# Row sums and reciprocals of a banded attention: products with ones against accumulating exponentials and transposed reciprocals

## The reference, cut to what matters

```python
def _L1_attn_ref(hidden_states, Wq, bq, Wk, bk, Wv, bv, Wo, bo):
    ...
    scores = jnp.einsum('bhtd,bhtwd->bhtw', q, kb) / scaling
    scores = jnp.where(valid[None, None], scores, -jnp.inf)
    probs = jax.nn.softmax(scores, axis=-1)
    ctx = jnp.einsum('bhtw,bhtwd->bhtd', probs, vb)
    ctx = ctx.transpose(0, 2, 1, 3).reshape(B, T, H * D)
    attn_output = ctx @ Wo.T + bo
    return attn_output
...
x = _layernorm(x + _L1_attn_ref(x, L1_attn_Wq, ...), axis=-1)
```

## Time and profile before

| | us |
|---|---|
| median of 3 runs | 878.39 |
| lowest, highest | 877.84, 883.13 |
| profiled execution, its own time | 879.82 |
| its span, first to last instruction | 878.0 |

### The profile page before, as it was taken

The page is one execution under the profiler, slowest core; times in us unless marked ns, Lnnn a source line. Parts: engine busy times, 40 slices in busy tenths (PEclk is TensorE's granted clock), DMA queues, the critical chain, the costliest instruction groups (busy, mean ns, idle before and its releaser), DMA issues.

```text
span 878.0 us, 20713 instructions
## 1 busy us (share of the span) xinstructions
PE 792.1 (90%) x7995; PEld 610.7 (70%) x7995; DVE 656.2 (75%) x1973; ACT 488.1 (56%) x1509; POOL 358.2 (41%) x604
## 2 busy tenths in 40 slices
PE   6888899988988889999988899999998899999992
PEld 4556777766666677766766778876766788877781
DVE  5363688687587878779667688789678788889576
ACT  3016335585646444577655554478656554578563
POOL 0358302304666532401685641311676632300655
PEclk9779989999989999999999999999999899999996
DMA  7892000000434100000126200000154100000001
GB/s 226 229 346 74 1 2 1 2 3 28 133 146 161 33 2 2 1 2 15 56 101 223 90 19 3 1 3 2 55 194 165 51 11 2 2 2 2 1 2 37
DMA packets 22994, 53.31 MB, mean 61 GB/s; under 512 B 3808, under 2 KB 9600, under 8 KB 22896
## 3 DMA queue, kind: packets, MB, share of 16 engines
q1 hardware_dynamic: 22896, 51.99, 17.9%
HBM read 48.67 MB, written 3.31 MB: 59 GB/s over the span
## 4 chain that ended last, share of the span: by engine, by line
PE 29%; DVE 10%; POOL 5%; ACT 4%; issue 2%; ACTq 0%; DVEq 0%; POOLq 0%
PE psum L441 6%; PE psum L436 6%; PE psum L478 5%; PE psum L621 2%; PE psum L643 2%; PE psum L634 2%; PE psum L464 2%; ACT x L701 1%; POOL rstd L1195 1%; DVE bn L937 1%; PE psum L471 1%; POOL xplus L1202 1%; PE psum L431 1%; PE psum L539 1%; PE psum L565 1%
## 5 line engine op out<-in xcount | busy, mean ns | idle before, releaser
L701 ACT ACTIVATE x<-res,ez,rstd 100x256 f32<-100x256 f32 x160 | 86.8, 593 | 67.4 <-POOL ez L1198 67.3
L1193 POOL TENSOR_SCALAR ve<-mv 100x2 f32<-100x2 f32 x96 | 22.2, 231 | 203.5 <-DVE mv L940 200.0
L478 PE MATMUL psum<-eT,ctx 128*128 128x100 f32 x768 | 101.2, 289 | 1.5 <-DVE eT L961 1.4
L478 PEld LDWEIGHTS psum<-eT,ctx 128*128 128x128 f32 x768 | 97.3, 205 | 3.7 <-DVE eT L961 2.7
L464 PE MATMUL psum<-ctxT,qT 128*100 128x361 f32 x256 | 84.1, 470 | 2.4 <-ACT qT L695 1.5
L695 ACT ACTIVATE eT<-psum 100x400 f32<-100x400 f32 (+3 forms) x128 | 61.8, 496 | 41.6 <-PE psum L471 18.2
L805 ACT ACTIVATE work<-psum,mx 100x100 f32<-100x100 f32 x256 | 67.4, 363 | 26.5 <-DVE mx L1104 26.2
L1177 POOL TENSOR_TENSOR kT<-cell,kT 100x722 f32<-100x722 f32 x12 | 20.6, 1719 | 137.9 <-ACT cell L675 137.9
L695 ACT ACTIVATE xT<-psum 128x400 f32<-128x400 f32 (+2 forms) x80 | 35.6, 447 | 70.7 <-PE psum L521 27.8
L811 ACT ACTIVATE work<-psum,mx 100x100 f32<-100x100 f32 x256 | 68.7, 386 | 8.6 <-DVE mx L1107 8.6
L1195 POOL TENSOR_TENSOR rstd<-ve,minus_half 100x2 f32<-100x2 f32 x96 | 69.7, 726 | 8.0
(11 more groups left out here) (241 smaller groups left out, 2007.7 us busy)
## 6 DMA issues: line engine op xcount, KB each, us to landing
ctx<-in_ctx SPq DMA_DIRECT2D x16, 768.0 KB, 7.0
ctxT<-in_ctxT SPq DMA_DIRECT2D x16, 722.0 KB, 5.4
cell<-in_cell SPq DMA_DIRECT2D x12, 282.0 KB
seq<-in_seq SPq DMA_DIRECT2D x12, 282.0 KB
x<-in_x SPq DMA_DIRECT2D x16, 200.0 KB
out<-vs SPq DMA_DIRECT2D x16, 200.0 KB
eT<-agent_rows SPq DMA_DIRECT2D x12, 200.0 KB
work<-in_x SPq DMA_DIRECT2D x4, 400.0 KB
```

Source lines behind the costliest of these rows:

```text
L478: last = e.matmul(bk[b][:, c * S:(c + 1) * S], s.ctx[:, b, j, c * P:(c + 1) * P], s.pT[:, b, j, :], start=j == 0, stop=j == S2C - 1)
L701: e.activation(dst[0:S, b, :], s.res[0:S, b, :], ACT.Identity, scale=s.rstd[:, b:b + 1], bias=s.shift[:, b:b + 1]).then_inc(*act.up(f"x{b}"))
```

## The change

The row sums are no longer made by PE. Each of the eight exponentials of an item now accumulates its row sum beside its output (`accum_out` into `s.den`). DVE takes the reciprocal of 100x8, POOL spreads it over 128 columns (`s.rspread`, which lies in the first half of `s.xT`), PE transposes that into bank 1, and DVE copies it to `s.xT[:, 1]`, from where the product L1116 takes it. The eight products with `sums` and the reciprocal of 128x100 go, as do the tile and its memsets. POOL's pieces for the four spreads stand between the stage's row addition and the masks of the next turn. The pieces are merged in new orders on all five engines: every string of ORDER is new.

```diff
-        sums = sb("sums", [S, 2, 2 * DH])
...
+                s.rspread = s.xT[0:S, :, :].rearrange("p c t -> p (c t)")[:, 0:P]
...
@@ tensor_turns, local
+                    e.wait_ge(*pool(f"re{i}", t))
+                    e.wait_ge(*dve(f"eT{i}", t))
+                    e.transpose(bk[1][:, 0:S], s.rspread, ident[0:S, 0:S]).then_inc(*pe.up(f"rt{i}"))
                     e.wait_ge(*act(f"eT{i}", t))
-                    e.wait_ge(*dve(f"eT{i}", t))
-                    for bank in range(2):
-                        for j in range(2):
-                            for r in range(ROWS):
-                                h = 2 * r + j
-                                last = e.matmul(bk[bank][32 * r:32 * r + 32, 0:S],
-                                                sums[:, j, :] if bank else s.v[0:S, b, c * HQ + h, :],
-                                                s.eT[0:S, h * S:(h + 1) * S], start=j == 0, stop=j == 1, skip_group_check=True)
+                    for j in range(2):
+                        for r in range(ROWS):
+                            h = 2 * r + j
+                            last = e.matmul(bk[0][32 * r:32 * r + 32, 0:S], s.v[0:S, b, c * HQ + h, :],
+                                            s.eT[0:S, h * S:(h + 1) * S], start=j == 0, stop=j == 1, skip_group_check=True)
                     last.then_inc(*pe.up(f"av{i}"))
...
@@ scalar_turns, local (and the same for heads 4 to 7)
                         last = e.activation(s.e[:, h, :], bk[0][0:S, h % 4 * S:(h % 4 + 1) * S], ACT.Exp,
-                                            bias=s.mx[0:S, h:h + 1])
+                                            bias=s.mx[0:S, h:h + 1], accum_out=s.den[0:S, h:h + 1])
...
@@ vector_turns, local
+                    e.wait_ge(*act(f"exb{i}", t))
+                    e.reciprocal(s.rden[0:S, 0:HQ], s.den[0:S, 0:HQ]).then_inc(*dve.up(f"rd{i}"))
                     e.wait_ge(*pe(f"trb{i}", t))
                     e.tensor_copy(s.eT[0:S, 4 * S:8 * S], bk[1][0:S, 0:4 * S]).then_inc(*dve.up(f"eT{i}"))
                     yield
+                    e.wait_ge(*pe(f"rt{i}", t))
+                    e.tensor_copy(s.xT[:, 1, 0:S], bk[1][:, 0:S]).then_inc(*dve.up(f"rT{i}"))
                     e.wait_ge(*pe(f"av{i}", t))
-                    e.reciprocal(s.xT[:, 0, 0:S], bk[1][:, 0:S]).then_inc(*dve.up(f"rd{i}"))
-                    e.wait_ge(*dve(f"rd{i}", t))
-                    e.tensor_tensor(s.aT[:, c, b * S:(b + 1) * S], bk[0][:, 0:S], s.xT[:, 0, 0:S], ALU.mult).then_inc(
+                    e.wait_ge(*dve(f"rT{i}", t))
+                    e.tensor_tensor(s.aT[:, c, b * S:(b + 1) * S], bk[0][:, 0:S], s.xT[:, 1, 0:S], ALU.mult).then_inc(
                         *dve.up(f"aT{i}"))
...
@@ gpsimd_turns, behind add_row of local, ahead of masks_product
+                for i in range(NB * NC):
+                    spread(s.gpsimd["local"], f"re{i}", s.vector["local"](f"rd{i}", t), s.rspread, S, HQ)
+                    yield
```

More of the change, by code:

```diff
@@ L70 @@
     "pick": "gates gath selT q k v hs0 hs tr0 tr1 av fo sc0 sc1",
-    "local": "xT q k v0 v1 " + " ".join(f"s{i} tra{i} trb{i} av{i}" for i in range(NB * NC)) + " out0 out1",
+    "local": "xT q k v0 v1 " + " ".join(f"s{i} tra{i} trb{i} rt{i} av{i}" for i in range(NB * NC)) + " out0 out1",
     "second": "xT q s0 s1 pT0 pT1 av0 av1 out0 out1",
@@ L89 @@
     "pick": "z0 z1 gp gt tie0 tie1 rk0 rk1 pk0 pk1 kT vs1 mx0 su0 mx1 su1 sm0 sm1 rd eT1 aT " + NORM,
-    "local": "k0 k1 k2 k3 v1 " + " ".join(f"ma{i} mb{i} eT{i} rd{i} aT{i}" for i in range(NB * NC)) + " " + NORM,
+    "local": "k0 k1 k2 k3 v1 " + " ".join(f"ma{i} mb{i} rd{i} eT{i} rT{i} aT{i}" for i in range(NB * NC)) + " " + NORM,
     "second": "mx0 nb0 mx1 nb1 pT0 rs aT1 " + NORM,
@@ L99 @@
     "pick": "zero re ve rstd nm0 nm1",
-    "local": "xb ve rstd nm0 nm1",
+    "local": "xb " + " ".join(f"re{i}" for i in range(NB * NC)) + " ve rstd nm0 nm1",
     "second": "xb prod qb ve rstd nm0 nm1",
@@ L850, in vector_agents @@
             e.memset(minus_half[:, :], -0.5)
-            for j in range(2):
-                for k in range(2):
-                    e.memset(sums[:, j, k * DH:(k + 1) * DH], float(j == k))
             e.memset(token_w, 0.0)
@@ L1415 @@
[L1415 to L1423 removed]
+        "ABCDABBCACBAADCBDABABACADBACBBDCDCCADDCDBDAAACBAABCBAADBCBACABDBACBCDBCDCABDDCADCABDACDABADABDCACBAC"
@@ new lines @@
+        "BABBBCDADCDCCCCBABACDADDADAADDCACBAABBBBBBDCBDCACABACADCCCCCDBAADBABBDACDDDDDABBCACCBBDCABDCDDCBCABD"
+        "CDACDADBACADBADBADCABCBDCACBCBDBDDAACBCDCCBADADBDABCBCDAABCABDBDCAABDDCCACABCDBDBCDABADCACBDCABDAAAA"
+        "ACDBCBDBCBBBCCADBDCACDCCDDDDDDBBCCDD"),
+    "DVE": (
+        "ABBDCCDDCAABAABBCADCBAACDBDABACABCDBCDDCCBAACDAABDBAADAABABBCCBBBABCDCCCDCCBDCDDADDDADAACABADCBCBBAD"
+        "ACCBBACDBBDCACBDCBAACBCBCDADCDABDCAABCBCACADBACADBDDBBCDBDDDAAACDACAABADBBADBBDBCCABCACBCCDDBDAACADB"
+        "DCDDCBABCBDAABDABACCABCDCACBABBCAADDBCBDCAABCDBAADBDCADBDBCDACBCCBDCCCDBDDDCADDDAACADBDABCABCACBCDBA"
+        "BCDBCABCCADDBADABDABCDBAADABCCDCDBABBCADAACDCBBDCBBCDAAADCCCDBDBAABADDDABBABCACADCBBCDBDCCBAADCDACDC"
+        "ADAABBBCDABDAACBCBCDAABCBCCBDDCCADACBDAABDAADBABDBDCCDBCBBACBCDDCCCBDDCDADDDCADAADBCBBABACABCCBADBAC"
+        "DBCDDABCAABCDDBBADCAADCABDCBCABDADBDACACBDCDCBBCBAADCDACCAAABBBADDADBDBBCCABCABCCDBCDADBAACDCDDACAAC"
+        "BBBDDAADBADCBCCABACBCBCBACDADCDABCADAADBDABBDBDBCCBBDACCBDCCDCCBDCDADDADDACADBADBACBBCAACCBDDBBCABDC"
+        "DAADCBCDBABCBADDAAABCDCBCBBDACADDCACBDBDCBCDDACACAADAADBBBDACCABCBBACBDDCCDBDDDBCDCDCD"),
@@ new lines @@
+    "ACT": (
+        "ABBBCACDBCAABAADBCABACCADDDDBCBCDAACDDBBACCADABBAABDCACABCBBADBDCACBADCCDBADABCDDABADCABCCDDCBDABABA"
+        "DCCCBBDBCCCDABBADCCACDBDADAABCCACBABADDDABABDDAAADABCBCBAABCBBBDACCCDDCBABDCCADABDADAADCCBADBCABDABD"
+        "BBCBBCCBDACACDCCAACBCDADBDBDCABDDABCDDCBABCADCADDBCABDCCBDADCBADABCDDBACDACABCCDDBACBDCBADACBBBCDDDC"
+        "CAAABDBBDACDACABCBADBDACACDAABCBAABDBCABDCBACDBBAABDCCDADDBCBCADCCADBADADBACDCABABBCAADDBBCBBABCDCAC"
+        "CACCADCBCDBADDDCDBCBDADADBCAABCDDACBBDCDBCDCBAACDBDAABCDDBDCCBAACDCADBBBACDADCACBBBDDACDABCCABBDDADA"
+        "ACCBBADCDDABCACABACABBABABACDDCBBADCABCCABDDDCBDCABCCADBADAABDACDCAADABCBDDCBABBBBBCADCCCDACADCACDCB"
+        "BDDCABBCDAADBDDACDBBCDCABDBDCACBDACCADBDDBCAADBAADCCBCDDCBBACBDACACDBBDDDBACCCABADBDBAACDACBCBDBDCDA"
+        "ACACABDBAADDBAABCCBABCCBABCCDCDADDCBDBDDDCCBDADCDBCD"),
@@ L1428 @@
+        "BABBCBCCACADADCDDBDABBADABCCCBBDCADDCCDDDBCADBAACBDCBACDBDCADBACBDCABADABCABCBDACCAADDBDBABCCCDBDDCD"),
     "SP": (
-        "ABCDAABCBAACDBDCDBCDAAABBABCDCDDCBCDAABCABDCBCDDABCD"),
+        "ABCDAACBBDCADCBADBCDABABACDBACDCDBCDAABBACCDDBCDBACD"),
 }
```

37 lines of the change are left out of this document (8 added, 29 removed).

## The result

The changed kernel took 899.55 us at the median of its runs (894.8 to 905.39), the kernel before 879.96 us beside it: ratio 1.0222, 95% interval 1.0175 to 1.027. The forecast was 872.0 us with a range that ended at 891. The profiled execution of the changed kernel took 894.8 us with a span of 892.7 us.

What follows compares the result with a forecast made beforehand. PE was taken to bound the kernel, with ACT close in the short local phases. Phase changes of -9.6 us plus 3.2 for the wait gave -6.4 from 878.39, so 872.0 us; range 858 to 891.

Steps and rivals of the forecast that it cites:

- ACT's gain in work: Local stage's exponentials: 512 accumulator reads at 0.09 us add 46.1 us to ACT, 11.5 us a phase.
- ACT I allow 0.94, the mean of its three best stretches: Four local phases: ACT can be busy 0.94 of a phase, so it needs 72.9, 59.1, 58.6 us in the first three.
- the forecast's own formula: Four local phases: each lasts as long as its neediest engine, busy time divided by the share allowed; together -9.6 us.
- rival B: Exponentials of L805 and L811: ACT becomes the local phases' bound, packing only to 0.84; +11.8 us, time 890; chance 0.30.
- B's turning point, 0.89: Local phases: if ACT packs to less than 0.89, they grow in sum; at 0.89 the four add to nothing.
- PE keeps its share: Local phases: PE keeps the busy share it has there now, 0.911 in phase 1, giving 85.2 us there.
- PE -14.1 us: Local items: dropped products with sums save PE 21.8 us, added transposes cost 7.7; net -14.1, bounds -16.0 and -6.4 per phase.
- rival C: Local phases: PE is not bound, weights load only 0.71, so its 14.1 us relief is slack; time 878; chance 0.13.
- The wait 3.2 us: PE's wait for POOL's spread ahead of the products: mostly covered, charged 3.2 us over 64 items; bounds 0 and 9.6.
- DVE -20.1 us: Local items: small reciprocal and copy replace the wide reciprocal, 20.1 us less DVE work over 64 items.
- The move of the masks at nothing: Next turn's masks, later in POOL's order, cost nothing; if cover went, DVE's 8.6 us wait would double at worst.
- time that changes outside the phases: Rest of the span: a change there, by the new orders, was named as another way of being wrong; no size.

Runs made afterwards that it cites:

- b_neworder: The work of the kernel before, put in the new orders of all five engines without POOL's spreads; ratio 1.0412, +36.2 us.
- a_noreads: The changed kernel in the new orders without the 512 accumulator reads, so the reciprocals are of wrong sums; ratio 1.011, +9.7 us.
- b_reads: The kernel before, old orders, with accumulator outputs added to its 512 exponentials, their sums unused; ratio 1.0328, +28.8 us.
- b_foursums: The kernel before, old orders, with four of the eight products with ones per item; ratio 0.9936, -5.6 us.
- a_noreads_old: The changed kernel's work without the 512 accumulator reads, put in the old orders; ratio 1.0048, +4.2 us.
- b_copyrecip: The kernel before, old orders, with a copy of the same shape in place of the wide reciprocal; ratio 0.997, -2.6 us.
- b_halfreads: The kernel before, old orders, with 256 accumulator reads added, on heads 4 to 7 only, unused; ratio 1.0088, +7.7 us.

## Why the prediction was wrong, point by point

**Sign and size.** In the old orders the steps of the change were worth: old way out -11.5, new way in +15.7, reads +33.6; the new orders then gave 18.3 back: +19.5 us. In the new orders, in which the change was measured, the reads are 9.8 us of the 19.5, and the new way of the reciprocals and the orders together the other 9.7. There the phases are long without the reads too: 328.3 us in the profile of b_neworder and about 308 in that of a_noreads, against 312.9 in the change. So in these orders it is not mainly the reads that make the phases long.

**ACT's gain in work: right.** 512 x 0.09 us; busy 537.5.

**What ACT's work costs: the step that failed.** It was "ACT I allow 0.94, the mean of its three best stretches". What this missed is seen in the old orders, where b_reads adds the reads alone. A whole phase has its items' chains, PE's scores, DVE's maxima, eight exponentials, PE's transposes, and over the four phases ACT packed to 0.79, in b_reads and in the change. No single phase of the two went over 0.84. With 0.79 in the forecast's own formula the phases need 68.5 / 0.79 = 86.7, then 70.4, 69.7 and 76.3 us: 303.1 in place of 277, +26, against +28.8 measured in b_reads. The 0.79 is read from b_reads itself, so this shows only that the step is large enough. It was rival B's mechanism. In the two phases that kept their clock ACT packed to B's own 0.84, inside the 0.8 to 0.9 that was named as B's sign. In the first two, with a lower clock, it packed to 0.72 and 0.79, and for that B had no term. B's turning point, 0.89, lay above what any phase has shown.

**PE keeps its share: wrong.** PE's share of the phases fell from 0.95 to 0.91 in b_reads. Even so the fall in share is only the idle time, 13.4 of the 28.4 us; 15.0 us are longer busy time for the same work, most of it at the lower clock (last section). Neither the forecast nor B had a term for that.

**PE -14.1 us: mis-sized.** The products were priced right (21.8). The transpose was put at 0.12 us, "near the lower end, since the products with v stand right behind it". It measured 0.24, the upper bound, in all items: net about -6.4 us, the bound of the other side. PE's relief does count, at about half (b_foursums), against rival C; so that error is worth some 4 us of time, by that estimate.

**The wait 3.2 us: too small.** The forecast held it covered "when POOL is free". POOL was busy in only 43% of the span, and PE still waited 21 times for the spread in the change, 14.8 us in all. Who waited for line L1212, us in total and times, of the change:

```profile
  PEld psum L639: 11.6, 15
  PE psum L639: 3.2, 6
```

After PE's relief is allowed for, a_noreads_old is left some 7 us slow. That lies inside the bounds of 0 and 9.6, by subtraction only.

**DVE -20.1 us: right, and worth little** (b_copyrecip: -2.6 us, at most 6, for 31 us). The rule of the Trainium skill, Perfetto Trace Analysis (Optimizing Scalar/DVE Operations), on the SBUF port that GpSimd and VectorE share was hardly put to the test: only one of the 64 small reciprocals ran while POOL spread. That one took 203 ns, and none took over 204, as the row of its line shows:

```profile
L1108 DVE RECIPROCAL rden<-den x64: 169/193/204, 146.0 to 841.6; 100x8 f32<-100x8 f32 x64
```

**Masks and orders.** The move of the masks at nothing stands: DVE's wait for their sum, 8.6 us before, was 3.2 us in the change. That new orders could be worth 18 us was in no case of the forecast. It did name time that changes outside the phases as another way of being wrong, and that came too: the rest of the span is 18 us shorter than before.

## What to carry to other kernels

Before moving work to a half idle engine, read how tightly it has ever packed over a whole stage whose chain runs through it, not over its best ten microseconds, and price the part beyond that share at full length; here 0.94 was the mean of the best stretches and 0.84 the best of any phase. A lone instruction costs its distance from start to start in the place where it stands; the same transpose held PE 0.24 us ahead of the products, and behind them 0.06 or less in half of the items. Where orders are written out by hand, a change and its orders are to be measured two by two, since each alone can look 4% bad.

## What the runs showed of the hardware that was not expected

PE's busy time hides a lower clock. b_reads gives PE the same work as the kernel before in the same orders. Windows of 10 us of b_reads, and the same of the kernel before:

```profile
170.00:180.00 10.00, 9.13 (x150) 6.14 (x149) 8.99 (x19) 6.88 (x39) 0.00 (x0) 1.00 0.01 2
...
190.00:200.00 10.00, 9.37 (x100) 6.35 (x96) 5.36 (x10) 6.69 (x39) 0.00 (x0) 0.50 0.01 3
```
```profile
170.00:180.00 10.00, 9.22 (x152) 6.32 (x152) 9.00 (x19) 5.41 (x22) 0.00 (x0) 1.00 0.01 2
...
190.00:200.00 10.00, 9.80 (x160) 6.88 (x160) 8.71 (x19) 7.43 (x29) 0.00 (x0) 1.00 0.01 2
```

At 190 us PE reads as 9.4 of 10 us busy in the one and 9.8 in the other, but with 100 matmuls against 160: the clock stood at 1.2 in place of 2.4 GHz all through. The two windows hold nearly, not exactly, the same stretch of the work. (The changed kernel has fewer matmuls in a phase to begin with, so its counts can't be compared in this way.) From 170 to 180 us, ahead of the fall, PE was about as busy in both kernels, 9.13 us against 9.22, so its busy share does not tell why the clock fell in the one alone. Times and clocks go together from run to run too: a_noreads took 880.4 us in a run at a mean clock of 0.983 and 892.8 in one at 0.959. In which stretches the clock falls differs between kernels with nearly the same waits (b_halfreads has 1.00 in all four phases, b_reads 0.90 and 0.93 in two), it fell in single phases without reads as well (0.88 in the second of a_noreads, 0.90 in the first of b_foursums), and no run here isolates what decides it. That part stays open.

The accumulator read shows 0.19 us or more as its own record (0.22 at the median of L805 in the change), and takes 0.09 us from ACT behind exponentials of 100x100, as it did behind copies of 100x256.
